# Attention passes: where the weights of a group lie, and one PSUM bank less for fetched rows

## The reference, cut to what matters

```
e     = leaky_relu(alpha_s[src] + alpha_d[dst] (+ alpha_edge in the first pass), 0.2)
m     = segment_max(e, dst)
w     = exp(e - m[dst])
denom = segment_sum(w, dst)
out   = segment_sum(w / denom[dst] * h[src], dst)        # h: 64 values, 16 for each head
```

## Time and profile before

| | before |
|---|---|
| median of 3 runs | 13124.66 us (13120.15 to 13129.22) |
| the profiled execution, its own time | 13120.87 us |
| its span, first to last instruction | 13119.1 us |
| POOL busy | 9811.0 us (75% of the span) |
| DVE busy | 7263.4 us (55%) |
| ACT busy | 4121.0 us (31%) |
| PE busy | 2341.8 us (18%) |
| POOL's indirect DMAs in the three attention passes (L2129) | 4209, busy 4299.4 us, 1284.1 us idle before them |
| first attention pass, POOL's first to last DMA start | 4687.7 to 6547.0 us |
| second | 6816.6 to 8673.2 us |
| third | 8943.1 to 10806.9 us |

### The profile page before, as it was taken

How to read it: one execution, slowest core, us unless ns; L and a number is a source line. 1 busy time by engine, 2 the same in 40 slices (tenths; PEclk the granted TensorE clock), 3 DMA queues, 4 the chain that set the end, 5 groups by cost and what they waited for, 6 DMA issues and landing times. The chain is left out here.

```text
span 13119.1 us, 196710 instructions
## 1 busy us (share of the span) xinstructions
PE 2341.8 (18%) x51836; PEld 1979.8 (15%) x51836; DVE 7263.4 (55%) x11947; ACT 4121.0 (31%) x4096; POOL 9811.0 (75%) x10026
## 2 busy tenths in 40 slices
PE   3000001200000243333223333313333320000001
PEld 1000000100000133333213222212332220000000
DVE  2777776377777544444434444444444446556656
ACT  4333333233333322121212111112111113666663
POOL 7777776777777677777777777777777776777775
PEclk9999999555555655555555555555555555555555
DMA  8445444344444222222212222222222223444443
GB/s 337 121 124 129 123 124 106 88 124 124 120 123 122 74 60 68 65 66 64 64 41 67 61 61 63 61 58 58 62 62 61 61 60 106 158 159 157 162 161 117
DMA packets 957876, 1318.90 MB, mean 101 GB/s; under 512 B 643852, under 2 KB 661427, under 8 KB 943088
## 3 DMA queue, kind: packets, MB, share of 16 engines
q10 hardware_dynamic: 547843, 802.76, 19.0%
q0 software_dynamic: 323648, 361.44, 14.2%
q1 hardware_dynamic: 85292, 141.67, 3.0%
HBM read 645.09 MB, written 659.95 MB: 99 GB/s over the span
## 5 line engine op out<-in xcount | busy, mean ns | idle before, releaser
L2129 POOL DMA_INDIRECT c_y<-g_tab,srcs x4209 | 4299.4, 1021 | 1284.1 <-issue 1284.1
L2624 POOL DMA_INDIRECT c_y<-h_tab,srcs x1547 | 1460.4, 944 | 506.4 <-issue 471.4
L1059 POOL DMA_INDIRECT c_y<-h_tab,srcs x1531 | 1444.7, 944 | 466.9 <-issue 466.9
L1059 POOL DMA_INDIRECT first_y<-h_tab,srcs x1452 | 1370.2, 944 | 444.9 <-issue 442.3
L2195 DVE TENSOR_TENSOR c_s<-c_y,c_ad 128x64 f32<-128x64 f32 x300 | 79.5, 265 | 2213.8 <-DMA c_y<-g_tab,srcs 2213.8
L475 PE MATMUL c_pb<-table,unit 128*128 x24576 | 764.2, 167 | 1607.6 <-issue 1607.6
L475 PE MATMUL c_pa<-table,unit 128*128 x24576 | 764.0, 167 | 1367.5 <-issue 1367.5
L475 PEld LDWEIGHTS c_pb<-table,unit 128*128 128x128 bf16 x24576 | 719.9, 103 | 1690.9 <-issue 1690.9
L475 PEld LDWEIGHTS c_pa<-table,unit 128*128 128x128 bf16 x24576 | 719.8, 103 | 1456.6 <-issue 1456.6
L2285 ACT ACTIVATE c_ex<-c_de 128x64 f32<-128x64 f32 x300 | 76.5, 255 | 2582.5 <-DVE c_de L2226 2582.1
L2240 DVE TENSOR_TENSOR_SCAN c_acc<-c_r,c_w_in 128x1156 f32<-128x1156 f32 x300 | 753.9, 2513 | 10.3
(11 more groups left out here) (447 smaller groups left out, 9224.6 us busy)
## 6 DMA issues: line engine op xcount, KB each, us to landing
c_y<-g_tab SPq DMA_DIRECT2D x12288, 0.3 KB
rows_d<-c_row ACTq DMA_DIRECT2D x96, 2048.0 KB
rows_d<-c_row ACTq DMA_DIRECT2D x288, 576.0 KB
c_q_raw<-q_start ACTq DMA_DIRECT2D x194, 776.0 KB, 6.1
rows_d<-c_row ACTq DMA_DIRECT2D x192, 784.0 KB
c_y<-h_tab SPq DMA_DIRECT2D x6144, 0.2 KB
q_start<-first_y SPq DMA_DIRECT2D x97, 776.0 KB, 8.8
c_y<-g_tab,srcs POOLq DMA_INDIRECT x4209
```

Source lines behind the costliest of these rows:

```text
L1059: nc.gpsimd.indirect_dma_start(y[:, g % NY, k, 0:D], None, h_tab, source(g, k))\
L2129: nc.gpsimd.indirect_dma_start(y[:, g % NY, k, :], None, g_tab, source(g, k))\
L2624: nc.gpsimd.indirect_dma_start(y[:, g % NY, k, :], None, h_tab, source(g, k))\
```

## The change

`ex` moves from SBUF to PSUM. In the first pass, where all eight banks are taken, it lies in the last 64 columns of the third bank of `r`, which the multipliers use up to column 1156. In the two other passes it has a bank of its own, and in exchange the second product bank (`z1`) goes: all passes now have one product bank. In the first pass the second exponential, that of the multipliers, no longer waits for the scan of the group before but for this group's own multiply, which reads `ex` out of a bank that the multipliers are written into.

```diff
-        de, ex, ex_bank = st.sb("de", [P, 2, H, GW]), st.sb("ex", [P, H, GW]), st.ps("z0", [P, 512])
+        de, ex_bank = st.sb("de", [P, 2, H, GW]), st.ps("z0", [P, 512])
...
-        other_bank = [] if bd is not None else [st.ps("z1", [P, 512])[:, 0:2 * TG]]
-        fetch = ColumnFetch(st, (pa, pb), [ex_bank[:, 0:2 * TG]] + other_bank,
+        shared = bd is not None
+        ex_at = r_banks[:, 1536 - H * GW:1536] if shared else st.ps("ex", [P, 512])[:, 0:H * GW]
+        ex = ex_at.rearrange("p (h t) -> p h t", h=H)
+        fetch = ColumnFetch(st, (pa, pb), [ex_bank[:, 0:2 * TG]],
...
                     act.activation(ex[:, :, 0:w], de[:, 1, :, 0:w], ACT.Exp).then_inc(exps.h, 1)
-                    act.wait_ge(*summed(pc.n))
+                    act.wait_ge(*(weighted[pc.b](pc.i + 1) if shared else summed(pc.n)))
```

## The result

The changed kernel takes 12802.94 us (median of 3 runs, 12802.21 to 12805.95) against 13124.66 before: a ratio of 0.9755, with a 95% interval from 0.9733 to 0.9778, or 322 us less. The profiled execution's span falls from 13119.1 to 12801.2 us, by 317.9. The forecast was 12811, with a range from 12792 to 12880.

A forecast was written before the change was run, and what follows sets the result against it. POOL's pace of issuing DMAs, stretched by DVE's multiply, was taken as the bound. Terms of -326, +9 and +3 us gave 12807 from the profiled 13120.87, and 3.8 more for the median gave 12811; range 12792 to 12880.

The forecast's parts named there:

- What bounds the kernel: Attention passes: POOL's own pace of issuing 1403 DMAs sets each pass's length; DVE, ACT and TensorE have slack.
- What stretches the DMAs: POOL stands still, once a group, while DVE's 2.01 us multiply takes both inputs from SBUF.
- rival B: DMAs stay stretched because the multiply's length or its writing to SBUF holds POOL: 13125 us, within 15; chance 0.06.
- The first term, 326 us: POOL's DMAs in three attention passes: all that their mean has above 0.944 us goes, 326.2 us together.
- SP late at the end, 9 us: Pass ends: SP, slightly slower than POOL's new pace, brings its last column late; 5, 4 and about 0 us.
- the tail of the wait, 3 us: First pass's end: scans 1.2 us later show only behind the last rows, one whole and three half pieces.
- The wait in the first pass, hidden: First pass: each of 100 scans comes 1.2 us later, covered by DVE's slack; 120 us without that cover.
- One product bank at no cost: Second and third pass: TensorE waits for DVE's choice; a 100.3 us round fits in POOL's 107.4, costed at 0.
- Rival A: A loop other than POOL's sets the pace; at 110 to 112 us a round, 12936 to 13030 us; chance 0.13.
- rival C: The single product bank makes TensorE and DVE take turns: 145 us a round, about 14000 us; chance 0.05.
- The sum: -326 + 9 + 3 = -314 us on the profiled 13120.87 gives 12807; the median, 3.8 above, gives 12811.
- The other signs: Attention passes: longest DMA about 1.1 us, mean 0.944 to 0.950, passes 103 to 112 us shorter, SP's slot waits nearly gone.

The follow-up runs named there:

- the fourth: The changed kernel with the first pass's weights in SBUF again and its multipliers' old wait, the other passes left changed: 12906.75 us, ratio 0.9836.
- fifth experiment: The changed kernel with `r` of the second and third pass in SBUF, so the scan there has both inputs in SBUF: 13124.35 us, ratio 1.0001.
- the third: The kernel before, with only the second exponential put behind the group's multiply in all three passes: 13116.3 us, ratio 0.9995.

## Why the prediction was right, point by point

*What bounds the kernel.* Right. POOL's DMAs lost 319.1 us and the span 317.9; with fewer of them the time falls by 1.249 us for each on the path, to within 2%.

*What stretches the DMAs.* Right, and now separated: with the place of an input changed, in either direction and at either of two instructions, the stretch goes or comes (the fourth and fifth experiment; the fourth takes back the first pass's wait as well, which costs nothing by the third). That the multiply's length or its writing to SBUF holds POOL (rival B) is refuted: both are as before, and nothing is stretched.

*The first term, 326 us.* It was 319 between the two profiled executions. Some 2 us of the missing 7 are mine: I had taken the median, 0.944 us, for the mean of a DMA without stretch. The other 5 belong to the execution of after, in which all of POOL's DMAs were about 1 ns longer: at L1059 in the second `conv` pass, which the change doesn't touch, they are 1446.6 us busy against 1444.7 before. In the execution with two banks, where that pass has 1444.7 us again, the 4209 take 3975.5 us, 323.9 less than before and 2.2 more than 4209 x 0.944.

*SP late at the end, 9 us, and the tail of the wait, 3 us.* Mis-sized: together they cost about 2 us. From POOL's last DMA of the first pass to its first of the second it was 269.6 us before and is 271.7 now; from the second to the third pass it is 269.9 both times. SP's pace was right: the first pass's third column began at 4799.44, and its last was out at 6415.2 below, so with 14 pairs and some 103 us for the last two, as in the working, a pair took 108.1 us where I had 108.3. The rows of after at the end of the first pass (the first is the rest of SP's last column from the view's start on), then of before:

```profile
6394.90 20.30 SPq L333 DMA_DIRECT2D c_y<-g_tab  x54
...
6416.24 0.27 DVE L2197 TENSOR_TENSOR c_s<-c_y,c_ad 128x64 f32<-128x64 f32 x1 [16.59 <-DMA c_y<-g_tab]
...
6438.33 0.94 POOL L2131 DMA_INDIRECT c_y<-g_tab,srcs  x1 [0.30 <-issue]
...
6443.13 0.17 DVE L2197 TENSOR_TENSOR c_s<-c_y,c_ad 128x12 f32<-128x12 f32 x1
```

```profile
6547.03 0.94 POOL L2129 DMA_INDIRECT c_y<-g_tab,srcs  x1 [0.30 <-issue]
...
6550.67 0.16 DVE L2195 TENSOR_TENSOR c_s<-c_y,c_ad 128x12 f32<-128x12 f32 x1
```

The last group with SP's rows did begin late, after DVE had waited 16.59 us for them. None of the four pieces behind it waits for rows, and the last piece began 3.9 us after POOL's last DMA was done (6443.13 against 6439.27). I had 6444.7 against 6439.7, and that 6444.7 came out so near is luck: SP was out 7 us earlier than worked out (6415.2 against 6422), and from there to the last piece it took 27.9 us where I had 22.7. But before the change the last piece also began 2.7 us after POOL's last DMA (6550.67 against 6547.97), because the half piece ahead of it takes DVE 4.95 us, longer than POOL needs for the three columns of the last one. My step set SP's chain against POOL's bare last DMA, and counted these 2.7 us as a cost of the change. New are 1.2 us in the first pass: the half piece now takes 5.79 us, with its scan 0.90 us late, and that is 0.84 of them. In the second and third pass the gap is 2.8 and 2.6 us, as before (2.7 and 2.6).

Two runs tell the tail from SP. With SP's columns short the first pass still has 3.7 us there, and 271.3 to the second pass, so in these executions SP's lateness is worth nothing and the 2 us are the late scans of the last pieces. The run with the wait alone in all three passes has them behind the first and behind the second, some 271.5 us to the next pass both times. But SP stood near the path. In the execution with `r` in SBUF, whose first pass is that of the change, SP's last column was out at 6421.3, the last piece began 8.0 us after POOL's last DMA and the second pass 275.4 us after it; there SP's lateness cost about 4 us.

*The wait in the first pass, hidden.* Right, and shown by itself: 288 times 1.2 us without effect in the kernel before. That was under the old pace of POOL, 114 us a round; under the new one the first pass is as short as the two that have no such wait, with the 2 us at its end.

*One product bank at no cost.* Right, and with more room than I had given it: I had 100.3 us for the round from the first pass, and the change shows 98.3 early in the first pass (steps at 4789.15 and 4887.40; why 2 us less isn't shown) and 96.4 in the second. Rival A (110 to 112) and rival C (145, taking turns) needed a longer round of TensorE and DVE than any that the rows show. TensorE does wait for L514 as foretold, and DVE before its lifts.

*The sum.* The terms were -326, +9 and +3; measured, -319, about 0 and about +2. The errors, 7 us on the first and 10 on the others, are opposite, so 12811 against 12803 looks better than the small terms were. What else moved lies where nothing was changed: 3.3 us less ahead of the first pass, 2.7 more behind the third. And the step from the profiled execution to the median, 3.8 us in the forecast, was none here: the profiled execution is the median. The other signs were there as put: the longest DMA at 1.1 to 1.2 us, the mean at 0.946, passes 104 to 110 us shorter, SP's waits for slots of the attention passes gone from the list of waits, where they were 131.0 us in 39 times before.

## What to carry to other kernels

When an engine that only issues DMAs is the bound, compare the longest of its instructions with the median before looking for waits: a stall inside an instruction shows as its length and not as idle time. Then look at what the neighbour was doing when a long one began, find the neighbour's instruction that does the same work without the effect (here the same multiply in another pass), and move the one operand by which the two differ. A wait or a lost buffer on the engines beside the bound can be costed at nothing only against their own pace, read where they run without the bound's cover. An offset at the end of a stage counts only by what it adds to the offset that was there before, and a few microseconds between two executions count only when a stage that the change doesn't touch stays as it was.

## What the runs showed of the hardware

POOL's hold ends with the single DVE instruction: two halves, 2.06 us together, leave a stretch of 132 us in all (4112.1 less 3980.3) where one of 2.0 us leaves 319. The expectation had left open whether POOL gets in between. And the hold isn't one of the multiply: under a scan of 2.57 us with both inputs in SBUF a DMA lasts up to 3.27 us. Wherever in the instruction a held DMA began, it ended at the same distance behind it: 0.76 to 0.78 us behind the multiply in the 292 long DMAs of the kernel before, as much behind a half, 0.75 to 0.76 us behind the scan. So the earlier in the instruction a DMA begins, the more it costs.
